# Operand pieces of two chunks: VectorE's work in the ramp of three attentions against work inside their slots

## The reference

```python
# layer 1: causal; layer 2: a bias by distance; layer 3: one added "void" key and a temperature
scores = einsum('bhqd,bhkd->bhqk', q, k) * scale   # + mask, or + bias
attn = softmax(scores, axis=-1)
out = einsum('bhqk,bhkd->bhqd', attn, v)
x = layernorm(x + out @ output_proj.T)
```

## Time and profile before

| | us |
|---|---|
| median of 3 runs | 1149.12 |
| lowest and highest run | 1142.61, 1151.37 |
| time of the profiled execution | 1147.93 |
| its span on the core | 1146.2 |
| TensorE busy | 987.9 (86%) |
| VectorE busy | 780.8 (68%) |
| ScalarE busy | 660.6 (58%) |
| GpSimd busy | 352.7 (31%) |

### The profile page before, as it was taken

One profiled execution on the slowest core, in us unless ns is written; L12 is line 12 of the kernel. 1 busy time (PEld: TensorE's weight loads), 2 busy tenths in 40 slices (PEclk: granted clock), 3 DMA queues, 4 the chain that ended last, 5 costly groups with the idle time before them and its releaser, 6 DMA issues.

```text
span 1146.2 us, 18859 instructions
## 1 busy us (share of the span) xinstructions
PE 987.9 (86%) x6456; PEld 500.3 (44%) x6517; DVE 780.8 (68%) x1663; ACT 660.6 (58%) x1282; POOL 352.7 (31%) x541
## 2 busy tenths in 40 slices
PE   5599889999988799366999999898899998988992
PEld 2267634544445588332333333476322222224661
DVE  5976686768742411489788887246888888855875
ACT  4664646566554355052667767575277766685451
POOL 7636510111442335420000000231111221645764
PEclk9799879999999899766999999989599999899997
DMA  5930224333621220333333210002234432311332
GB/s 142 171 73 1 93 102 140 129 119 106 174 79 31 65 64 17 89 94 107 100 122 123 80 65 31 2 1 93 99 112 146 132 99 77 110 29 46 98 102 84
DMA packets 98375, 101.70 MB, mean 89 GB/s; under 512 B 13354, under 2 KB 80571, under 8 KB 98199
## 3 DMA queue, kind: packets, MB, share of 16 engines
q1 hardware_dynamic: 86169, 89.28, 26.6%
q0 software_dynamic: 6432, 8.18, 2.5%
q10 hardware_dynamic: 5680, 3.04, 1.0%
HBM read 66.60 MB, written 38.09 MB: 91 GB/s over the span
## 4 chain that ended last, share of the span: by engine, by line
PE 66%; DVE 18%; issue 5%; ACT 5%; POOL 4%; DMA 2%; SPq 0%; another core or an unknown queue 0%; ACTq 0%; POOLq 0%; DVEq 0%
PE PS L894 13%; PE PS L878 13%; PE PS L851 8%; DVE negm L1696 5%; PE PS L705 5%; PE PS L700 5%; PE PS L1063 3%; PE PS L1073 3%; PE PS L1193 3%; PE PS L881 3%; PE PS L854 2%; PE PS L902 2%; ACT arena L1323 2%; PE PS L1208 2%; DVE X L1551 1%
## 5 line engine op out<-in xcount | busy, mean ns | idle before, releaser
L1323 ACT ACTIVATE arena<-PS 128x512 f32<-128x512 f32 (+3 forms) x768 | 362.5, 548 | 187.9 <-PE PS L881 121.1
L1696 DVE TENSOR_REDUCE negm<-PS 128x2 f32<-128x1024 f32 (+3 forms) x384 | 404.7, 1087 | 89.2 <-PE PS L851 44.5
L878 PE MATMUL PS<-arena 128*128 128x512 bf16 (+3 forms) x707 | 219.8, 363 | 8.4 <-ACT arena L1323 5.1
L894 PE MATMUL PS<-arena,VPAD 128*32 128x512 f32 (+3 forms) x1536 | 188.1, 561 | 0.1
L851 PE MATMUL PS<-arena 32*128 32x512 bf16 (+3 forms) x768 | 144.3, 374 | 29.5 <-DVE negm L1696 25.9
L851 PEld LDWEIGHTS PS<-arena 32*128 32x128 bf16 x768 | 36.4, 91 | 213.4 <-DVE negm L1696 106.9
L878 PEld LDWEIGHTS PS<-arena 128*128 128x128 bf16 x768 | 69.7, 98 | 120.3 <-issue 57.1
L2533 POOL CAST nmp<-negm 128x16 bf16<-128x16 f32 x48 | 9.4, 196 | 360.7 <-DVE negm L1696 241.1
L700 PE MATMUL PS<-arena,W 128*128 128x512 f32 x144 | 84.1, 719 | 12.4 <-ACT arena L1241 9.9
L705 PEld LDWEIGHTS PS<-W,arena 128*128 128x128 f32 x640 | 80.0, 204 | 14.0 <-issue 7.1
L705 PE MATMUL PS<-W,arena 128*128 128x128 f32 x640 | 81.6, 288 | 3.0 <-DVE arena L1640 2.7
(11 more groups left out here) (335 smaller groups left out, 1538.1 us busy)
## 6 DMA issues: line engine op xcount, KB each, us to landing
arena<-score_q SPq DMA_DIRECT2D x48, 288.0 KB
arena<-score_k SPq DMA_DIRECT2D x48, 288.0 KB
arena<-max_parts SPq DMA_DIRECT2D x48, 256.0 KB
max_parts<-arena SPq DMA_DIRECT2D x36, 256.0 KB, 2.9
score_k<-arena SPq DMA_DIRECT2D x36, 128.0 KB
score_q<-arena SPq DMA_DIRECT2D x12, 384.0 KB
arena<-rows_y SPq DMA_DIRECT2D x16, 256.0 KB, 3.9
arena<-slots SPq DMA_DIRECT2D x46, 65.0 KB, 1.9
```

The source lines that it names most:

```text
L878: mm = pe.matmul(PS[:, b, q0:S], OK[s][:, r, kt * P:(kt + 1) * P], OQ[s][:, r, q0:S], start=True, stop=True)
L894: mm = pe.matmul(PS[32 * r:32 * r + 32, 7, q0:S], VP[:, u, kt, r, :], PB[:, kt % 2, r, q0:S], start=(kt == 0), stop=True, skip_group_check ...
L1323: act.activation(PB[:, kt % 2, r, q0:S], PS[:, 4 + use % 3, q0:S], ACT.Exp, scale=slope(u % G, r) if o["slope"] else 1.0).then_inc(exped, 1)
L1696: vec.tensor_reduce(negm[:, u % 2, 2 * rp:2 * rp + 2, qt], PS[:, 2 * (use % 2):2 * (use % 2) + 2, 0:nk], AX.X, ALU.max, negate=True).then_ ...
```

## The change

The three piece instructions of chunks 2 and 3 are no longer in the ramp. Each goes alone to the head of a slot, ahead of that slot's `maxima`. The steps of chunks 0 and 1 stay. In the combine ramp, `values` of chunks 3 and 2 also stand after fewer ramp slots (6 and 10, before 10 and 13); in the other two ramps the string is the same and its `split` of chunks 2 and 3 is empty.

```diff
+SPLIT_SLOTS = {2: (2, "lo"), 8: (2, "mid"), 14: (2, "low"), 24: (3, "lo"), 30: (3, "mid"), 38: (3, "low")}
 SPILL_SLOTS = {1: (1, 0), 6: (1, 1), 22: (2, 0), 30: (2, 1), 46: (3, 0), 54: (3, 1)}
...
-LAYER0_VECTOR = words("ss xn decay memory y x1 ss2 xn2 tot ln t.xn ssp t.tot t.ln split values")
+LAYER0_VECTOR = words("ss xn decay memory y x1 ss2 xn2 tot ln t.xn ssp t.tot t.ln prep values")
...
-COMBINE_VECTOR, COMBINE_VECTOR_TURNS = words("tot ln split values"), "001103321201RR3RRRRRRRR32RRR2R"
+COMBINE_VECTOR, COMBINE_VECTOR_TURNS = words("tot ln prep values"), "001103321201RR3RRRR32RRRR2RRRR"
...
-LAYER2_VECTOR, LAYER2_VECTOR_TURNS = words("o.tot o.ln c.tot c.ln split values scores"), "1310203211002021310103RRRRRR2R2RRR3R323RRR"
+LAYER2_VECTOR, LAYER2_VECTOR_TURNS = words("o.tot o.ln c.tot c.ln prep values scores"), "1310203211002021310103RRRRRR2R2RRR3R323RRR"
...
+            def piece(c, tag, step):
+                L = lanes[c]
+                if step == "lo":
+                    vec.wait_ge(*A.at(c, tag + ".k"))
+                    vec.tensor_tensor(L.pair, L.pair, L.parts[:, :, 0, :], ALU.subtract).then_inc(*V.did(c, tag + ".lo"))
+                elif step == "mid":
+                    vec.wait_ge(*V.at(c, tag + ".lo"))
+                    vec.tensor_copy(L.parts[:, :, 1, :], L.pair).then_inc(*V.did(c, tag + ".mid"))
+                else:
+                    vec.wait_ge(*V.at(c, tag + ".mid"))
+                    vec.tensor_tensor(L.parts[:, :, 2, :], L.pair, L.parts[:, :, 1, :], ALU.subtract).then_inc(*V.did(c, tag + ".low"))
+
             def splits(c, tag):
...
+                for step in ("lo", "mid", "low"):
+                    piece(c, tag, step)
...
-                    elif step == "split":
-                        splits(c, "p1")
+                    elif step == "prep":
+                        if c < 2:
+                            splits(c, "p1")
...
                 def slot(t):
+                    if t in SPLIT_SLOTS:
+                        c, step = SPLIT_SLOTS[t]
+                        piece(c, f"p{a + 1}", step)
                     if max_job(t) is not None:
                         maxima(max_job(t))
```

More of the change, by code:

```diff
@@ L96 @@
 NORM_G = "{0}.va {0}.rs"
-PREP_V = "{0}.lo {0}.mid {0}.low {0}.v"
+PREP_V = ("{0}.lo {0}.mid {0}.low {0}.v", "{0}.v {0}.lo {0}.mid {0}.low")
 EXPERTS_A = " ".join(f"x{r}.xT x{r}.xT4 " + " ".join(f"x{r}.h{i}" for i in range(8)) for r in range(2))
 EXPERTS_T = " ".join(f"x{r}.tr " + numbered(f"x{r}.f", 8) + (" x1.o0 x1.o1 x1.o2" if r else "") + f" x{r}.o x{r}.o4" for r in range(2))
-VECTOR_STEPS = words(" ".join([
+VECTOR_STEPS = [words(" ".join([
     "m.ss m.xn m.cl m.cut m.heads m.cut0 m.pre m.inv m.u m.uu m.mem m.qn m.y0 m.y1 m.y2 m.y m.x1 m.ss2 m.xn2",
-    "m.t m.tot", NORM_V.format("m"), "t.rcp t.xn t.ssp t.rcp2 t.tot", NORM_V.format("t"), PREP_V.format("p1"),
+    "m.t m.tot", NORM_V.format("m"), "t.rcp t.xn t.ssp t.rcp2 t.tot", NORM_V.format("t"), PREP_V[late].format("p1"),
     "o1.tot", NORM_V.format("o1"), "r1.lg sh.t sh.y x0.y x0.y4 x1.y0 x1.y1 x1.y2 x1.y x1.y4",
-    "cb.a cb.tot", NORM_V.format("cb"), PREP_V.format("p2"),
-    "o2.tot", NORM_V.format("o2"), "ch.tot", NORM_V.format("ch"), PREP_V.format("p3"), "p3.vs",
+    "cb.a cb.tot", NORM_V.format("cb"), PREP_V[late].format("p2"),
+    "o2.tot", NORM_V.format("o2"), "ch.tot", NORM_V.format("ch"), "p3.lo p3.mid p3.low p3.v p3.vs" if not late else "p3.v p3.vs p3.lo p3.mid p3.low",
     "o3.tot o3.bn o3.mv r3.lg o3.ln",
-    "e.first e.tot", NORM_V.format("e")]))
+    "e.first e.tot", NORM_V.format("e")])) for late in (False, False, True, True)]
 SCALAR_STEPS = words(" ".join([
@@ L170, in __init__ @@
         self.sems = [sem(f"{engine}_chunk{c}") for c in range(B)] + [sem(f"{engine}_whole")]
-        self.order = [[name for name in chunk_steps if c == B - 1 or name not in last_only] for c in range(B)] + [whole_steps]
+        steps = chunk_steps if isinstance(chunk_steps[0], list) else [chunk_steps] * B
+        self.order = [[name for name in steps[c] if c == B - 1 or name not in last_only] for c in range(B)] + [whole_steps]
         self.number = [{name: i + 1 for i, name in enumerate(steps)} for steps in self.order]
@@ L1552, in normalised @@
                 t.then_inc(*V.did(c, tag + ".ln"))
-            def splits(c, tag):
[L1555 to L1561, removed]
+            def piece(c, tag, step):
[9 more added lines that the diff above has]
+                    vec.tensor_tensor(L.parts[:, :, 2, :], L.pair, L.parts[:, :, 1, :], ALU.subtract).then_inc(*V.did(c, tag + ".low"))
+            def splits(c, tag):
+                for step in ("lo", "mid", "low"):
+                    piece(c, tag, step)
             def head_values(c, tag, bias=None):
@@ L2008, in combine_and_prep @@
                         normalised(c, L.tot, L.X, "cb")
-                    elif step == "split":
-                        splits(c, "p2")
+                    elif step == "prep":
+                        if c < 2:
+                            splits(c, "p2")
                     else:
@@ L2032, in layer2 @@
                         normalised(c, L.tot, L.X, "ch")
-                    elif step == "split":
-                        splits(c, "p3")
+                    elif step == "prep":
+                        if c < 2:
+                            splits(c, "p3")
                     elif step == "values":
```

## The result

The changed kernel takes **1142.1 us** (median of 7 runs, 1137.74 to 1144.92) against 1149.08 for the kernel before beside it: ratio 0.9957, 95% interval 0.9936 to 0.9978, which is 4.9 us less (2.5 to 7.4). It was run on two more occasions, with 0.9944 (0.9925 to 0.9964) and 0.9952 (0.9931 to 0.9973). The forecast was 1146.7, 2.4 us less, and "within 1%". The profiled execution took 1142.1 us with a span of 1140.4.

What follows compares the result with a forecast made beforehand. TensorE was taken to fill the score slots and VectorE the ramp; ramp gains of 2.8, 1.4 and 0.3 us less slot costs of 2.15 gave -2.4 us, 1149.12 to 1146.7 us, range 1140 to 1152.

Steps and rivals of the forecast that it cites:

- First ramp, 2.8 us: First attention's ramp: slot 0's scores start 2.8 us sooner, at least 1.8, at most 6.3.
- first triple: First ramp: removing chunk 2's three pieces frees 1.8 us, not 3.1, since TensorE's fill comes later.
- second triple: First ramp: removing chunk 3's three pieces ahead of job 12 gives 1.0 us at slot 0.
- rival A: Ramps: TensorE's clock comes up sooner and stays full, gaining 6 us, to 1140.7; chance 0.13.
- Rival D: Ramps: a DMA, the row of maxima, sets slot 0, so only the costs stay, 1151.3; chance 0.10.
- Second ramp, 1.4 us: Second attention's ramp: scores start at 536.0 instead of 537.4, 1.4 us gained, ends 0 and 6.3.
- the idle time foreseen: Second ramp: VectorE idles about 3 us ahead of job 3, waiting for TensorE's fill.
- Third ramp, 0.3: Third attention's ramp: VectorE's wait for a TensorE product grows to 3 to 4 us; gain 0.3, ends 0 and 3.
- Slots: Score slots: pieces cost 0.8 us in the first attention, 0 in the second, 1.35 in the third; 2.15 in all.
- GpSimd at slot 2: Slot 2: GpSimd's instructions meet the new `lo` and end about 1 us later; the sum stays.
- The sum: Whole kernel: gains of 4.5 us less costs of 2.15 us make 2.4 us less, 1146.7 us.
- the tenth that I had set: Windows around the ramps: a clock change of more than a tenth would show the forecast wrong.

Runs made afterwards that it cites:

- first_chunk2: Kernel before, with only chunk 2's pieces of the first attention moved to slots 2, 8, 14; ratio to the kernel before 0.998, 2.3 us less.
- none: Changed kernel with each piece only 8 columns wide, so wrong scores; ratio to the kernel before 0.9942.
- slots4: Changed kernel with pieces in slots 4, 8, 12, 28, 30, 36 and TensorE's chunk 2 projections later in the second ramp; ratio to the kernel before 0.9979.
- mix: Changed kernel with later second-ramp projections, third attention's pieces in its ramp, the others in slots 2, 8, 14, 28, 30, 36; ratio to the kernel before 0.9943.
- only_first: Kernel before, with only the first attention's pieces of chunks 2 and 3 moved to slots; ratio to the kernel before 0.9974, 3.0 us less.
- double: Changed kernel with each piece made twice in its slot, about 19.5 us more VectorE work; ratio to the kernel before 1.0121.

## Why the prediction was right, and where its sizes were not

**First ramp, 2.8 us: the number at slot 0 came out, its second part by luck; short by slot 8.** 14.2 became 11.2 to 11.4. The first triple's 1.8 us, VectorE's own chain, is confirmed by `first_chunk2` (12.41). The second triple's 1.0 us is the right number for a wrong reason. The sum let TensorE make the value projection at half clock and the scores follow the fill of job 14 directly: fill at 10.5 us after the common start. The clock stayed full, and the fill came at 8.8; then the scores waited 1.76 us for the row of maxima, a wait that the sum did not have in this ramp. The two errors, a fill placed 1.7 us too late and a wait of 1.76 us left out, cancel. By slot 8 the gain is 26.0 - 21.9 = 4.1 us on average. The 1.2 us more are the step that was mis-sized: rival A's mechanism came about in this one ramp. The clock in 160 to 170 us is 0.59 to 0.61 in the three traces with the pieces in the ramp and 0.83 to 1.00 in the six without that the table counts, and the slow start of the scores is shorter. But it is not tied to the pieces alone: `none`, `slots4` and `mix`, which have none in this ramp either, show 0.73, 0.69 and 0.67. Rival D's wait came about too, the row of maxima sets slot 0, but only after the 2.8 us had been gained.

**Second ramp, 1.4 us: right on its own clock course, and not what is left at the end.** TensorE's clock goes through this ramp in one of two ways. The traces of the kernel before, `first_chunk2`, `none`, `slots4` and the third run of the changed kernel have the one, the others the second. In the first way slot 0 moved from 25.4 to 23.98, 1.4 us, and the idle time foreseen is there, in the changed kernel's third trace:

```profile
511.87 2.52 PE L702 MATMUL PS<-arena,W 128*128 128x512 f32 x4
...
514.74 3.49 DVE L1706 TENSOR_REDUCE negm<-PS 128x2 f32<-128x1024 f32 x3 [2.97 <-PE PS L853]
```

On the second, in its second trace:

```profile
514.23 3.62 PE L702 MATMUL PS<-arena,W 128*128 128x512 f32 x4
...
518.43 3.49 DVE L1706 TENSOR_REDUCE negm<-PS 128x2 f32<-128x1024 f32 x3 [4.40 <-PE PS L853]
```

There the gain at slot 0 is 1.1 us. What then counts is when the clock is back at full: in the first way slot 8 is 2.4 us sooner (40.7 to 38.25), in the second 0.3 (40.5 to 40.2), since scores that start sooner only run longer at half clock. That both ways happen with and without the pieces (the trace before has the first, `only_first` the second) says that the pieces don't choose between them. What does is not settled.

**Third ramp, 0.3: right.** On the same clock course 28.15 became 27.6 to 27.7 at slot 0, 0.5 us, and 41.3 became 40.95 at slot 8, 0.35 us.

**Slots.** First attention 0.8 foreseen, 0.6 to 0.8 paid on average, but as 0.3 in the unit of slot 38 in every trace and 0.4 ahead of it in four of six (0.7 and 0.8 in two), where I had nearly none and 0.7. Second 0, right to 0.01 us. Third 1.35 foreseen, 0.75 paid in four traces and 0.9 and 1.2 in two: the units of slots 14, 24 and 38 grew by 0.08, 0.25 and 0.42, where I had 0.45 each. The output step in the middle of a unit takes more of a delay than I gave it.

**GpSimd at slot 2**: its cast took 1.12 us where 0.19 is its median, the lateness of about 1 us that was foreseen, and no turn waited for it. The Trainium skill (SBUF — State Buffer, section "Who interferes with whom") has VectorE's two-input instruction block GpSimd's reads, and the trace agrees: the cast ended with VectorE's `lo`.

**The sum.** With the means of the table: first attention -4.1 + 0.6 = -3.5 (ramp and slots to 48), second -0.3 or -2.4 by the clock course, third -0.35 + 0.75 = +0.4. That is 3.4 or 5.5 us less. Measured on three occasions: 4.9, 6.4 and 5.5. My 2.4 lay low by the 1.2 of the first ramp's clock and by the 0.6 that I charged too much for the third attention's slots; on one clock course of the second ramp it lay low there too, on the other high. One part of the traces' difference is not the change's: the expert stage behind the first attention takes 172.3 to 173.6 us in eight traces and 174.7 to 176.0 in six, with no relation to where the pieces are, and the trace before has 175.3 while that after has 172.7. So 2.6 us of the 5.8 between those two spans are that stage's two lengths, whose cause stays open, as does how often each clock course comes.

**What would have proved it wrong.** The clock of the window 520 to 540 moved by 0.16 and that of 160 to 170 by 0.23, more than the tenth that I had set. For the first ramp that was the right alarm: the term held at slot 0, and what the clock made of it by slot 8 did not. For the second it is in part a false one, since the ramp lies earlier in the changed kernel's traces: the third of them has the clock course of the kernel before and still shows 0.57 in this window. The idle times ahead of fills in slots 2 to 45 stayed far below 3 us; only `double` brought the 3.2 us shown above.

## What to carry to other kernels

Work that is taken out of a ramp is worth what the other engine isn't late by, step by step, and the first transfer that had been hidden is the next bound; ask what traffic is still moving when it is issued, not only when it is issued. A total that comes out may hide two errors, so compare each step of the sum with its row. Slack in a ring of buffers is used up at once and not in shares: the first 18.8 us of VectorE's work cost 1.5, the same again some 20, a third of it by TensorE's lower clock after its waits; and its place is not where the engine idles but where the other engine is last to want the buffers. Where a ramp runs with a changing clock, compare traces of the same clock course, and measure after the clock is back at full.

## What the runs showed of the hardware that was not expected

- One program goes through the same ramp with TensorE's projection at 2.52 or 3.62 us, and comes out of it 2 us apart (38.3 and 40.2 us to slot 8); in the third attention 39.1 and 41.0.
- A row of 8 KB from on-chip memory to on-chip memory is waited for 5.0 us after GpSimd's queue issued it and 5.6 us after SyncE's did: another queue did not make it faster. Issued 8.0, 6.2 and 5.6 us after the same common step, it was there after 10.9, 11.1 and 11.2 us, each time when earlier loads had drained.
- TensorE's clock can fall within the score slots too: with VectorE's work doubled, TensorE was busy 3.39 of the 5 us from 195 to 200, and its clock was 0.84 there and 0.82 in the next 5 us, against 1.00 in the changed kernel.
- On one chip the last stage, behind the third attention, took 131 us instead of 116, in all four kernels, and slots 48 to 127 of the first attention 115 to 117 us instead of 109 to 113.
